# Two chained adapters and MLP layers: another order at the turn between the two MLPs, and the second batch's residual in two transfers with a semaphore each

## The reference

```python
q, k, v = x @ Wq, x @ Wk, x @ Wv
attn_out = softmax(q @ k.T * V ** -0.5) @ v @ Wp + bp
cms_out = gelu(attn_out @ cW1 + cb1) @ cW2 + cb2 + one_hot(target_codes)
modifier = gelu(concat([attn_out, cms_out]) @ mW1 + mb1) @ mW2 + mb2
x = clip(x + cms_out + modifier, 0, 1)
h = gelu(x @ W_down[role] + b_down[role]) @ W_up[role] + b_up[role]
x = layernorm(x + h) * gamma[role] + beta[role]
```

## Time and profile before

| | |
|---|---|
| median of three runs | 2125.99 us (2125.24 to 2126.84) |
| profiled execution | 2125.54 us |
| its span | 2123.9 us |
| PE busy | 2075.0 us, 98% |
| DVE busy | 1601.6 us, 75% |
| ACT busy | 1095.0 us, 52% |
| POOL busy | 712.2 us, 34% |
| granted TensorE clock | 0.998 |

### The profile page before, as it was taken

One profiled execution on the slowest core, in us unless ns is written; L12 is line 12 of the kernel. 1 busy time (PEld: TensorE's weight loads), 2 busy tenths in 40 slices (PEclk: granted clock), 3 DMA queues, 4 the chain that ended last, 5 costly groups with the idle time before them and its releaser, 6 DMA issues.

```text
span 2123.9 us, 24970 instructions
## 1 busy us (share of the span) xinstructions
PE 2075.0 (98%) x9112; PEld 1696.9 (80%) x9112; DVE 1601.6 (75%) x1927; ACT 1095.0 (52%) x1623; POOL 712.2 (34%) x694
## 2 busy tenths in 40 slices
PE   8999999999999999999999999999999999999997
PEld 6887887888787887888887888788888888878884
DVE  4357877767867877876886887877686888787776
ACT  5256635544447654544554755444454666354444
POOL 1244415664001331766100232455400032155520
PEclk9999999999999999999999999999999999999999
DMA  8895444444212424444403222422130423411211
GB/s 301 230 230 148 131 115 116 117 125 99 107 62 87 152 74 127 110 124 102 127 30 131 84 73 73 106 60 60 40 129 1 149 70 99 120 60 50 60 60 40
DMA packets 184137, 221.94 MB, mean 104 GB/s; under 512 B 10304, under 2 KB 148288, under 8 KB 180560
## 3 DMA queue, kind: packets, MB, share of 16 engines
q1 hardware_dynamic: 175488, 184.58, 26.8%
q0 software_dynamic: 7296, 29.47, 7.7%
q10 hardware_dynamic: 1232, 6.29, 0.8%
HBM read 199.33 MB, written 62.91 MB: 123 GB/s over the span
## 4 chain that ended last, share of the span: by engine, by line
PE 81%; DVE 10%; DMA 3%; ACT 3%; issue 2%; SPq 0%; ACTq 0%; DVEq 0%
PE bank L852 27%; PE bank L854 27%; PE bank L853 26%; DVE ring L1698 2%; DMA xs<-pc 1%; DMA fold_staging<-fold_w 1%; DVE pc L1865 1%; DVE lsum L2143 1%; ACT ring L1253 1%; DVE xa L1735 1%; DVE vc L1740 1%; DMA stage<-ready_up 1%; DVE pc L1967 1%; ACT raw L1396 1%; PE bank L1221 0%
## 5 line engine op out<-in xcount | busy, mean ns | idle before, releaser
L1698 DVE TENSOR_TENSOR ring<-stage,ring 128x1024 fp32r<-128x1024 f32 (+1 forms) x288 | 371.1, 1300 | 91.4 <-ACT ring L1253 90.7
L852 PE MATMUL bank<-xa,ring 128*128 128x512 f32 x1016 | 396.5, 390 | 2.6 <-DVE xs L2101 2.1
L854 PE MATMUL bank<-xa,ring 128*128 128x512 f32 x1016 | 395.4, 389 | 0.0
L853 PE MATMUL bank<-xa,ring 128*128 128x512 f32 x1016 | 395.4, 389 | 0.0
L1253 ACT ACTIVATE ring<-stage 128x1024 fp32r<-128x1024 f32 (+1 forms) x288 | 271.3, 963 | 121.8 <-PE bank L854 66.0
L852 PE MATMUL bank<-ph_hi,ring 128*128 128x512 f32 x808 | 317.5, 393 | 7.0 <-issue 2.4
L854 PE MATMUL bank<-ph_hi,ring 128*128 128x512 f32 x808 | 314.6, 389 | 0.0
L853 PE MATMUL bank<-ph_lo,ring 128*128 128x512 f32 x808 | 314.5, 389 | 0.0
L852 PE MATMUL bank<-vc,ring 128*128 128x512 f32 x704 | 275.1, 391 | 7.3 <-DVE ring L1698 5.8
L853 PE MATMUL bank<-vc,ring 128*128 128x512 f32 x704 | 274.0, 389 | 0.0
L854 PE MATMUL bank<-vc,ring 128*128 128x512 f32 x704 | 274.0, 389 | 0.0
(11 more groups left out here) (185 smaller groups left out, 3613.5 us busy)
## 6 DMA issues: line engine op xcount, KB each, us to landing
stage<-ready_up SPq DMA_DIRECT2D x40, 896.0 KB, 5.2
stage<-mod_w SPq DMA_DIRECT2D x112, 256.0 KB, 3.5
stage_pair<-ready_pair SPq DMA_DIRECT2D x12, 1792.0 KB, 10.2
stage<-mod_w SPq DMA_DIRECT2D x28, 512.0 KB, 5.1
ready_up<-ready_up POOLq DMA_DIRECT2D x100, 128.0 KB, 5.0
ready_up<-cms_w SPq DMA_DIRECT2D x98, 128.0 KB, 3.7
ready_pair<-cms_w SPq DMA_DIRECT2D x42, 256.0 KB, 6.9
fold_staging<-fold_w SPq DMA_DIRECT2D x16, 512.0 KB, 5.4
```

The costliest lines, as they stand in the source:

```text
L852: pe.matmul(dst, lh, rh, start=start and n == 0, stop=False, skip_group_check=not start)
L853: pe.matmul(dst, lh, rl, start=False, stop=False, skip_group_check=not start)
L854: done = pe.matmul(dst, ll, rh, start=False, stop=n == last, skip_group_check=not start)
L1698: dve.tensor_tensor(ring_part(key, 1), staged(key), f32(ring_part(key, 0)), ALU.subtract).then_inc(w_lo, 1)
```

## The change

Four things are moved or split. "The sibling" of the short name is a kernel that isn't needed here; the diff is against the kernel before.

1. **POOL, `residual`:** batch 0 goes in one transfer of 1 MB after its last addition (`res_first`), instead of two of 512 KB. Batch 1 still goes in two, each with a semaphore of its own (`res_second[0]`, `res_second[1]`), instead of one for both.
2. **T4:** its hi on ACT waits for the first half of batch 1 only. Its lo leaves `cms_end`, goes into DVE's `slot8` and waits for the second half.
3. **ACT's order:** A's hi (slot 9, group 0) and the copy of part C's Q1 to `snap` are taken ahead of T4's hi. C's hi comes ahead of gelu 0, and D's hi (group 0 of slot 8's down weights) comes from `seven_slot(9)` into `slot8`, ahead of gelu 2.
4. **DVE's order:** A's lo first, then the Q2 addition, T4's lo, the Q6 addition, C's lo; B11's lo comes ahead of the second Q7 addition; D's lo comes at the end of `slot8`.

TensorE's and SP's queues stay as they are.

```diff
+        res_first, res_second = sem("res_first"), [sem(f"res_second{half}") for half in range(2)]
...
-                for m in (0, 2):
+                if b == 0:
+                    pool.wait_ge(added, added_at(r, CH - 1, b, KT - 1))
+                    pool.dma_start(xs[:, b, :, :], pc[:, b, :, :], accum_op=ALU.add).then_inc(res_first, 16)
+                    return
+                for half in range(2):
+                    m = 2 * half
                     pool.wait_ge(added, added_at(r, CH - 1, b, m + 1))
-                    pool.dma_start(xs[:, b, m:m + 2, :], pc[:, b, m:m + 2, :], accum_op=ALU.add).then_inc(res_added[b], 16)
+                    pool.dma_start(xs[:, b, m:m + 2, :], pc[:, b, m:m + 2, :], accum_op=ALU.add).then_inc(res_second[half], 16)
...
             def slot8(r):
                 n = CH
-                act.wait_ge(prod_done, prod8_at(r, 1, Q1))
-                act.activation(snap[:, 0, :], bank[BANK8[Q1]][:, :], ACT.Copy).then_inc(snapped, 1)
-                split_hi((r, "A", n + 1, 0))
+                act.wait_ge(prod_done, prod8_at(r, 1, Q6))
+                split_hi((r, "C", n + 1, 0))
                 act.wait_ge(combined, comb8_at(r, C11_8))
                 gelu(r, n, 0, raw[:, 0, :])
                 operand_b_hi(r, n, B11)
-                act.wait_ge(prod_done, prod8_at(r, 1, Q6))
-                split_hi((r, "C", n + 1, 0))
+                act.wait_ge(prod_done, prod8_at(r, 1, Q4))
+                split_hi((r, "D", n, 0))
...
-                act.wait_ge(res_added[0], 32 * (r + 1))
+                act.wait_ge(res_first, 16 * (r + 1))
                 operand_hi(vc, T3, raw[:, 0:2, :], cms_hi)
+                act.wait_ge(prod_done, prod8_at(r, 0, Q6))
+                split_hi((r, "A", CH + 1, 0))
+                act.wait_ge(prod_done, prod8_at(r, 1, Q1))
+                act.activation(snap[:, 0, :], bank[BANK8[Q1]][:, :], ACT.Copy).then_inc(snapped, 1)
                 act.wait_ge(cms_t, t0 + CMS_T[T4])
-                act.wait_ge(res_added[1], 32 * (r + 1))
+
+                act.wait_ge(res_second[0], 16 * (r + 1))
...
-                dve.wait_ge(cms_lo, (r + 1) * BUILDS)
+                split_lo((r, "A", n + 1, 0))
+                dve.wait_ge(cms_lo, t0 + BUILT[T3])
                 dve.wait_ge(snapped, snap_at_(r, n, 0))
                 combine8(Q2, raw[:, 0, :], snap[:, 0, :])
-                split_lo((r, "A", n + 1, 0))
+                dve.wait_ge(res_second[1], 16 * (r + 1))
+                operand_lo(vc, T4, raw[:, 2:4, :], cms_hi, t0 + BUILT[T4], cms_lo)
+                dve.wait_ge(cms_lo, (r + 1) * BUILDS)
                 combine8(Q6, raw[:, 2, :], snap[:, 0, :])
+                split_lo((r, "C", n + 1, 0))
...
-                split_lo((r, "C", n + 1, 0))
                 combine8(Q7, raw[:, 1, :], raw[:, 2, :])
+                hidden_lo(r, n, B11)
                 combine8(Q7, raw[:, 3, :], raw[:, 3, :])
                 dve.wait_ge(combined, comb8_at(r, U3_8))
                 combine8(Q4, raw[:, 1, :], raw[:, 1, :])
-                hidden_lo(r, n, B11)
+                split_lo((r, "D", n, 0))
```

More of the change, by code:

```diff
@@ L385, in build @@
         hid_sum = sem("hid_sum")
-        res_added = [sem(f"res_added{b}") for b in range(GROUP)]
+        res_first, res_second = sem("res_first"), [sem(f"res_second{half}") for half in range(2)]
         z_ready, z_hi, z_lo = (sem(n) for n in ("z_ready", "z_hi", "z_lo"))
@@ L1420, in seven_slot @@
                 last = n in LASTS
-                split_hi((r, "D", n - 1, 0))
+                if n > CH + 1:
+                    split_hi((r, "D", n - 1, 0))
                 split_hi((r, "A", n, 1))
@@ L1811, in slot8 @@
             def slot8(r):
-                n = CH
+                n, t0 = CH, r * BUILDS
                 def combine8(q, to, other):
@@ L1844, in seven_add @@
                 else:
-                    dve.wait_ge(res_added[b], 32 * (r + 1))
+                    if b == 0:
+                        dve.wait_ge(res_first, 16 * (r + 1))
+                    else:
+                        dve.wait_ge(res_second[m // 2], 16 * (r + 1))
                 minus = q in (Q5, Q7, Q4)
@@ L1895, in seven_slot @@
                 last = n in LASTS
-                split_lo((r, "D", n - 1, 0))
                 if n > CH + 1:
+                    split_lo((r, "D", n - 1, 0))
                     seven_add(r, n - 2, Q2)
@@ L2074, in cms_end @@
                 operand_lo(vc, T3, raw[:, 0:2, :], cms_hi, t0 + BUILT[T3], cms_lo)
-                operand_lo(vc, T4, raw[:, 2:4, :], cms_hi, t0 + BUILT[T4], cms_lo)
             def mod_end(r):
```

## The result

The changed kernel takes **2109.96 us** (median of four runs, 2108.99 to 2110.63), the kernel before 2125.61 beside it (median of four, 2124.41 to 2126.84); the ratio is 0.9926, with a 95% interval of 0.9909 to 0.9943. The forecast was 2112.0, range 2109.5 to 2119. The profiled execution took 2110.63 us for a span of 2108.9, against 2125.54 and 2123.9 before.

What follows compares the result with a forecast made beforehand. TensorE was taken to bound the kernel, busy 2075.0 of 2123.9 us. Turn excess 15.6 less 4 x 0.4 for the remaining wait gives 14.0 us: profiled 2111.5, forecast 2112.0 us, range 2109.5 to 2119.

Steps and rivals of the forecast that it cites:

- the 15.6 us: TensorE's excess at the turn from part C's first matmul to Q2's first, over four rounds: all that shorter waits could win.
- The cause in ACT's queue: T4's hi on ACT waits for the residual transfer until 323.71, with Q1's copy and A's hi queued behind it.
- The estimate of the 1 MB transfer: Batch 0's joined transfer on POOL, costed from the same bytes in two pieces (11.9 us), landing at about 315.3.
- The bound of 32 us: Upper bound for the 1 MB transfer, from 256 KB in 8.1 us within memory; T3's product would stall 14 us a round.
- The waits for T4, A, C and D: TensorE's waits for these lo halves at the turn would go; C had 1.5 us to spare, D 0.7.
- The wait that stays: TensorE's wait before down Q6 for T2's lo: 0.25 us, 0.4 a round with its slow restart.
- The shared ports: DVE's splits and POOL's addition hinder each other before T2: between the full 15.6 us and 0.7 us less per round.
- The 2.0 us for A's split: Time taken for A's split of 768 columns on DVE, to its end at 337.70 in the kernel before.
- 1 (the waits move): Waits at the turn shrink but a later step is late by 1 to 2 us a round: 2116.4 us; chance 0.16.
- 2 (the lead given back): TensorE loses the turn's lead later, to something keeping its own time: 0 to 4 us left, about 2123.5; chance 0.08.
- 3 (DVE in front of the third transfer): DVE waits with C and D behind it; slower from a landing at 327.6, 4 us per further us; chance 0.05.
- 4 (the third issue held): POOL's third residual issue is held, costing 0.4 x 4: 2113.6 us; counted inside the forecast's 0.70.

Runs made afterwards that it cites:

- run 1: The kernel before with only the new order on ACT and DVE, residual transfers and semaphores as before: 2113.72 us, ratio 0.9953 to before.
- run 2: The changed kernel's three transfers and split T4 waits, with the order of ACT and DVE as in the kernel before: 2116.76 us, ratio 0.9966 to before.
- run 3: The changed kernel with D's split put back at the head of slot 9 on ACT and DVE: 2113.20 us, ratio 0.9949 to before.
- run 8: The changed kernel with A's second split moved behind B22 on ACT and behind T1 and B22 on DVE: 2109.47 us, ratio 0.9930 to before.
- run 7: The changed kernel with a useless 2 MB copy ahead of the last residual transfer: 2127.13 us, ratio 1.0011 to before.
- the four transfers: The changed kernel with batch 0's residual in two halves again, so four transfers: 2110.23 us, ratio 0.9932 to before.
- runs 1 and 5: The first: the kernel before with only the new order on ACT and DVE, 2113.72 us; the second: the changed kernel with batch 0's residual in two halves again, 2110.23 us.
- runs 6 and 7: The changed kernel with a useless copy ahead of the last residual transfer, 1 MB in the first, 2 MB in the second: 2115.40 and 2127.13 us.

## Why the prediction was right, step by step

**What bounds it and the 15.6 us.** Right: the turn gave back 14.4 us of the profiled execution's 14.9, and the four rounds, which had differed by 1.8 us, became alike.

**The cause in ACT's queue.** Right, and it could be cured from either side: by the order (run 1) or by the transfers (run 2). The text's "one queue order" is too narrow for rounds 0 and 1, where with the new order alone T4's hi still waits for a held transfer.

**POOL.** The third issue isn't held. It comes at 311.18 and its data land at 321.62, which is 311.5 and 321.9 with the shift of 0.29 us between the two traces; forecast were 311.2 and 322 to 323. The estimate of the 1 MB transfer (the same bytes in two pieces, 11.9 us) was near: 10.6 to 11.3. The bound of 32 us, from transfers within memory, was far off. One reading of before was wrong without harm: the shortest time to landing, 8.2 us, is that of the fourth transfer, not of the first, which landed at 312.12 and not at 311.3. The landings were thus 3.8 us apart and not 3.1, within the 3 to 4 us that the forecast used. That the third issue would not be held was read from one row of before; it proved right, but no cause for the hold was known, and none is now.

**The waits for T4, A, C and D.** Gone in all rounds, as forecast. The prediction counts from part C at 317.05; with the shift of 0.29 that is C's hi at 324.05 (324.1), C's lo 325.15 (325.15), D's lo 330.01 (330.0), T2's lo ending at 337.55 (337.6). T4's lo, at 321.9, came just ahead of the 322 to 324 given as a sign. Queue order plus durations from rows of before gave a timeline to 0.1 us here, where the order was known and nothing outside it (a transfer, a new collision of DVE and POOL) decided.

**The wait that stays.** Right in place, and its size is the one term that was mis-sized: 0.29 us a round and not 0.4, so 0.4 us less in all. The pause is 0.19 us (0.42 between the starts, where 0.23 is normal) and was forecast as 0.25; the restart behind it costs 0.08 where I had added 0.15. With 15.6 - 1.2 = 14.4 instead of 14.0 the profiled forecast of 2111.5 becomes 2111.1; the profile shows 2110.6, of which 0.3 us was gone before the first turn. The median is 0.7 below the profiled execution, where I had put it 0.5 above; that difference lies within the spread of the runs and isn't explained by the working.

**The shared ports.** The 2.0 us for A's split were 1.58 plus a wait of 0.39 for ACT, the same end. POOL's T3 addition took 1.82 as in before, and 1.30 in the one run (3) where DVE's split came after it. The Trainium skill, SBUF — State Buffer, section "SBUF: two separate sides", has the one that starts first hold the ports for its whole length; the changed kernel and run 8 agree, as POOL's additions that started inside a split ended 1.15 and 1.16 us after it, and A's split, started inside an addition, 0.82 after that (alone they take 1.30 and 0.94). What I hadn't seen is that this couples the end of A's split to POOL's chain: moving a DVE instruction there moves only the collision.

**Rivals.** 1 (the waits move) didn't come; it is what the transfers alone do, with waits for C, D and T2 of 1.6 to 2.0 us a round. 2 (the lead given back) is refuted by the distance from round to round. 3 (DVE in front of the third transfer) is a real mechanism, of which the changed kernel stays clear by 1.4 us. I put its break-even at a landing of 327.6, through down Q1. By the law above it is where the excess is 3.9: S = 6.25 + 3.6 = 9.9, or 326.9 in the times of before, 0.7 earlier, for it is down Q6 that suffers first. With the clock's fall, which three rounds of run 7 show on top, it would be earlier still, at S = 9.0 with 0.84 us more in every round; no round between 8.06 and 9.60 shows where the fall begins. 4 (the third issue held) wasn't so; its price, by the four transfers, is 0.6 us and not 1.6 in all.

## What to carry to other kernels

A change that touches one instruction's wait and the order around it can be priced to about a tenth of a microsecond a round by walking each queue forward with durations from the trace, with each step's latest start on the engine that bounds written beside it. It held for the changed kernel and run 1; run 3, where a collision of DVE and POOL went away, was priced 0.7 us a round too high, and run 2 was 0.2 to 0.6 too low. When a wait is put into an in-order queue, look for the price at the far end of the chain behind it, not at the first consumer: here 13 us later. And two remedies for one wait don't add: 11.7 and 8.5 us alone, 14.4 together.

## What the runs showed of the hardware

- Of POOL's accumulating transfers within the core's memory three were issued without a hold. Ahead of a fourth, with the same bytes in all, POOL was idle 4.9 to 5.1 us (before and runs 1 and 5), about 1 us of it for its data, and the issue came 0.33 to 0.38 us after the second transfer's landing in all 12 rounds. With a plain copy as the third of four (runs 6 and 7) the fourth wasn't held.
- 1 MB in one such transfer landed 10.6 to 11.3 us after its issue in the changed kernel, 512 KB 6.6 to 11.0 in the kernel before. It isn't a fixed time: the first packet moved some 4.6 to 4.8 us after the first issue, with SyncE's loads filling the DMA engines until then, and from there the three or four transfers shared one stream, 2 MB in 12.6 us in round 0 of the changed kernel. How much of the first 4.6 us is the other queue's load isn't shown.
- A plain copy of 1 MB on the same queue made T4's lo start 2.7 us later in round 0, one of 2 MB 5.0 (2.6 to 3.3 and 5.0 to 5.7 in the four rounds).
- TensorE's granted clock fell to half for about 3 us after pauses near 3 us (2.9 to 3.8 us between starts), in three rounds of four, at about 0.84 us each; the fourth, with 3.44 between starts, kept its clock.
